# Cross-attention over 1500 keys: key tiles walked in pairs, the turned maxima between two attended tiles, one addition fewer on GpSimd

## What is computed

```python
def sdpa(q, k, v, causal):
    scale = 1.0 / np.sqrt(q.shape[-1])
    scores = jnp.einsum('bhqd,bhkd->bhqk', q * scale, k)
    p = jax.nn.softmax(scores.astype(jnp.float32), axis=-1).astype(q.dtype)
    return jnp.einsum('bhqk,bhkd->bhqd', p, v)
```

## Time and profile before

| what | value |
|---|---|
| median of 3 runs | 1476.83 us (1475.7 to 1477.4) |
| the profiled execution's own time | 1476.38 us |
| its span in the trace | 1474.6 us |
| PE busy over the span | 1403.8 us, 95% |
| DVE, ACT, POOL busy | 906.7, 581.3, 553.7 us |
| the stage that the change touches | from 160.8 to 560.5 us |
| one batch of it, from T to T | 24.52 us, thirteen times out of fifteen |

### The profile page before, as it was taken

The page is one execution under the profiler, slowest core; times in us unless marked ns, Lnnn a source line. Parts: engine busy times, 40 slices in busy tenths (PEclk is TensorE's granted clock), DMA queues, the critical chain, the costliest instruction groups (busy, mean ns, idle before and its releaser), DMA issues.

```text
span 1474.6 us, 20618 instructions
## 1 busy us (share of the span) xinstructions
PE 1403.8 (95%) x7850; PEld 740.6 (50%) x7851; DVE 906.7 (61%) x1429; ACT 581.3 (39%) x880; POOL 553.7 (38%) x385
## 2 busy tenths in 40 slices
PE   6979899999999989998998999999999999999998
PEld 3446555555555544444654455555344355555344
DVE  6896766666667616421226788887433778888540
ACT  1264366666666652001442344444122434444121
POOL 2630388888888891000001144452000144453000
PEclk9999999999999999999999999999999999999999
DMA  7000623232323204004842011110042001110000
GB/s 274 0 2 20 165 70 90 67 92 71 88 66 92 52 13 191 0 0 174 335 124 71 0 39 39 40 39 1 0 122 70 1 27 39 39 39 13 1 0 25
DMA packets 45019, 95.62 MB, mean 65 GB/s; under 512 B 6860, under 2 KB 28892, under 8 KB 44908
## 3 DMA queue, kind: packets, MB, share of 16 engines
q1 hardware_dynamic: 44912, 94.21, 21.0%
HBM read 72.04 MB, written 0.97 MB: 50 GB/s over the span
## 4 chain that ended last, share of the span: by engine, by line
PE 84%; DVE 8%; POOL 3%; issue 2%; ACT 2%; DMA 0%; SPq 0%; DVEq 0%; ACTq 0%; POOLq 0%
PE psum L1658 23%; PE psum L2175 10%; PE psum L1899 5%; PE psum L1875 5%; PE psum L1849 4%; PE psum L2107 4%; PE psum L1832 3%; PE psum L2138 3%; PE psum L1818 3%; POOL XN L708 3%; PE psum L2165 2%; PE psum L2170 2%; DVE WA L1341 2%; PE psum L2167 2%; PE psum L2166 2%
## 5 line engine op out<-in xcount | busy, mean ns | idle before, releaser
L1341 DVE TENSOR_REDUCE WA<-psum 112x2 f32<-112x1000 f32 x192 | 229.8, 1200 | 89.9 <-PE psum L1849 89.9
L708 POOL TENSOR_TENSOR XN<-XN,WBZ 125x896 f32<-125x896 f32 x128 | 266.5, 2082 | 16.8 <-POOL XN L708 0.9
L1052 ACT ACTIVATE WA<-psum,y_bias 125x448 f32<-125x448 f32 x192 | 118.6, 633 | 208.9 <-PE psum L2170 190.4
L933 ACT ACTIVATE WBZ<-psum 125x896 f32<-125x896 f32 x192 | 175.5, 915 | 43.9 <-PE psum L1875 33.3
L2175 PE MATMUL psum<-WA,ctxN 125*128 125x448 f32 x384 | 180.9, 554 | 0.8 <-ACT WA L1052 0.7
L740 POOL TENSOR_TENSOR XN<-const,y_max 112x896 bf16<-112x896 f32 x32 | 75.2, 2350 | 246.2 <-DVE y_max L1557 189.2
L731 POOL TENSOR_SCALAR ctxT<-ctxT 128x375 f32<-128x375 f32 x32 | 56.2, 1756 | 250.9 <-ACT std L806 248.4
L1557 DVE CUSTOM_DVE_ANT_0 XA<-psum,WA 112x375 bf16<-112x375 f32 x240 | 125.3, 541 | 37.6 <-PE psum L2138 36.6
L1875 PE MATMUL psum<-R 100*125 100x224 f16 x768 | 110.7, 266 | 0.0
L1570 DVE RECIPROCAL WBZ<-WBZ 128x224 f32<-128x224 f32 x68 | 105.1, 1546 | 0.1
L1875 PEld LDWEIGHTS psum<-R 100*125 100x125 f16 x768 | 78.9, 136 | 28.3 <-issue 25.0
(11 more groups left out here) (255 smaller groups left out, 2337.9 us busy)
## 6 DMA issues: line engine op xcount, KB each, us to landing
R<-WA SPq DMA_DIRECT2D x192, 93.8 KB, 2.2
WA<-in_ctxT SPq DMA_DIRECT2D x14, 750.0 KB, 4.3
ctxT<-in_ctxT SPq DMA_DIRECT2D x11, 750.0 KB, 4.2
ctxN<-in_ctx SPq DMA_DIRECT2D x32, 192.0 KB, 2.5
ctxT<-in_ctxT SPq DMA_DIRECT2D x32, 187.5 KB, 2.4
R<-in_ctx SPq DMA_DIRECT2D x7, 768.0 KB, 7.3
R<-in_ctxT SPq DMA_DIRECT2D x7, 750.0 KB, 7.2
WA<-in_ctx SPq DMA_DIRECT2D x6, 768.0 KB, 6.4
```

The lines of the kernel that those rows point to most:

```text
L708: nc.gpsimd.tensor_tensor(z_sum[b % 2][0:TK, :], first[0:TK, :], z_p[t % 4][0:TK, :], ALU.add)\
L933: nc.scalar.activation(z_p[t % 4][0:TK, :].rearrange("p (k n) -> p k n", k=2), psum[0:TK, s:s + 2, 0:2 * GC], ACT.Exp, scale=float(CHD0) * ...
L1052: nc.scalar.activation(y_pT[t][0:TK, g * HALF:(g + 1) * HALF], bank[2 + u % 3][0:TK, 0:HALF], ACT.Exp, bias=y_bias[0:TK, bass.ds(b * NT + ...
L1341: V.tensor_reduce(z_mx[0:PR, r:r + 3:2, c], psum[0:PR, lo:lo + 2, 0:PC], AX_X, ALU.max)\
```

## The change

PE now takes two tiles at a time: S of the next two tiles, U, A of tile t, A of tile t+1, and then one piece of V or K whose two halves have the second U between them. In the pair of tiles 8 and 9, T stands between the two A, and both K halves come behind the second U. The four Z of a batch stand directly behind the last A, no longer with a K half in them. POOL adds one tile fewer (SUMS = 8), and PE sums one more (ADDED = 4). POOL's `divide` moves behind the first addition of the next batch. ACT and DVE follow the same pairs.

```diff
-        VALUES_AT = {0: (0, 0), 1: (0, 1), 2: (1, 0), 3: (1, 1), 4: (2, 0), 5: (2, 1)}
-        KEYS_AT = {6: (0, 0), 7: (0, 1), 9: (1, 0), 10: (1, 1), 11: (2, 0), 12: (2, 1)}
+        VALUES_AT = {0: 0, 2: 1, 4: 2}
+        KEYS_AT = {6: 0, 8: 1, 10: 2}
         TURN_AT = 8
-        SUMS = NT - 3
+        SUMS = NT - 4
...
             for b in range(B):
-                if b > 0:
-                    divide(b - 1)
                 if b > 1:
                     pool.wait_ge(sem("z_added"), ADDED * (b - 1))
                 for t in range(1, SUMS + 1):
+                    if b > 0 and t == 2:
+                        divide(b - 1)
...
-                    if b > 0 and t == 3:
+                    if b > 0 and t == 4:
                         quotient(b - 1)
...
             exps(0, 0)
+            exps(0, 1)
             for b in range(B):
...
+                for t in range(0, NT, 2):
+                    for u in (t + 2, t + 3):
+                        if u < NT:
+                            exps(b, u)
+                        elif b + 1 < B:
+                            exps(b + 1, u - NT)
+                        if b + 1 < B and t == TURN_AT and u == t + 2:
+                            shifts(b + 1)
+                    if t + 2 == NT:
+                        evacuate(b)
+                    if b + 1 < B and t in VALUES_AT:
+                        values(b + 1, VALUES_AT[t])
+                    if b + 2 < B and t in KEYS_AT:
+                        high_keys(b + 2, KEYS_AT[t])
...
+                for t in range(0, NT, 2):
+                    for m, k in ahead(b, t) + ahead(b, t + 1):
                         maximum(m, k)
                         if k == UNITS - 1:
                             combine(m)
...
+                    if b + 2 < B and t in KEYS_AT:
+                        low_keys(b + 2, KEYS_AT[t])
+                    if b > 0 and t == 2:
                         invert(b - 1)
...
+            scores(0, 1)
             for b in range(B):
...
+                for t in range(0, NT, 2):
+                    units = ahead(b, t) + ahead(b, t + 1)
+                    for u in (t + 2, t + 3):
+                        if u < NT:
+                            scores(b, u)
+                        elif b + 1 < B:
+                            if b + 1 == EARLY and u == NT:
+                                pe.wait_ge(sem("z_queries1"), STACKED)
+                            scores(b + 1, u - NT)
+                    for m, k in units[0:1]:
                         unit(m, k)
+                    attended(b, t)
                     if b + 1 < B and t == TURN_AT:
                         turn_maxima(b + 1)
...
+                    for m, k in units[1:-1]:
+                        unit(m, k)
+                    attended(b, t + 1)
...
+                    if t + 2 == NT:
+                        for x in range(ADDED):
+                            sums(b, x)
+                    if t == TURN_AT:
+                        for m, k in units[1:][-1:]:
+                            unit(m, k)
+                    for side in range(2):
+                        if b + 1 < B and t in VALUES_AT:
+                            values(b + 1, VALUES_AT[t], side)
+                        if b + 2 < B and t in KEYS_AT:
+                            keys(b + 2, KEYS_AT[t], side)
+                        if side == 0 and t != TURN_AT:
+                            for m, k in units[1:][-1:]:
+                                unit(m, k)
```

More of the change, by code:

```diff
@@ L1373, in _ @@
             for b in range(B):
-                for t in range(NT):
-                    for m, k in ahead(b, t):
+                for t in range(0, NT, 2):
+                    for m, k in ahead(b, t) + ahead(b, t + 1):
                         maximum(m, k)
@@ L1378, in _ @@
                             combine(m)
-                    if b + 2 < B and t in KEYS_AT and KEYS_AT[t][1] == 1:
-                        low_keys(b + 2, KEYS_AT[t][0])
-                    if b > 0 and t == 3:
+                    if b + 2 < B and t in KEYS_AT:
+                        low_keys(b + 2, KEYS_AT[t])
+                    if b > 0 and t == 2:
                         invert(b - 1)
-                if b + 2 < B:
-                    low_keys(b + 2, PIECES - 1)
             invert(B - 1)
@@ L1941, in _ @@
             warm(6, 4)
+            scores(0, 1)
             for b in range(B):
-                for t in range(NT):
-                    for m, k in ahead(b, t)[0:1]:
+                for t in range(0, NT, 2):
[8 more added lines that the diff above has]
+                    for m, k in units[0:1]:
@@ L1962, in _ @@
-                    attended(b, t)
                     if b == B - 1 and t >= COOL:
                         warm(7, 1)
[L1965 to L1969, removed]
+                    for m, k in units[1:-1]:
+                        unit(m, k)
+                    attended(b, t + 1)
+                    if b == B - 1 and t + 1 >= COOL:
+                        warm(7, 1)
```

## The result

The changed kernel took 1467.07 us in the median of four runs (1465.4 to 1470.41), the kernel before 1477.12 beside it: a ratio of 0.9936, 95% interval 0.9917 to 0.9955. Forecast were 1464.5 and 1458.5 to 1471.5. The profiled execution took 1470.41 us, the longest of the four.

A forecast was written before the change was run, and what follows sets the result against it. PE was taken as the bound, busy 24.18 of 24.50 us a batch. Savings of 9.4 + 3.3 - 0.4 = 12.3 us from 1476.38 gave 1464.1; with the median 0.45 above, 1464.5 us, range 1458.5 to 1471.5.

The forecast's parts named there:

- PE sets the pace, by its changes of layout: Steady batch: PE busy 24.18 of 24.50 us; each change between three layouts costs; pairs with V fall from 3.72 to 3.61.
- Pair 8, T at 0.38, in A's layout: Pair of tiles 8 and 9: T between two A shares their layout and costs 0.38 us; pair sum 3.77.
- The rival of a layout of its own: At T between the two A: T's own layout adds 0.20 us a batch, 2.8 in all, 1467.3; chance 0.12.
- an A behind an A takes no more than the price: Denies the rival that A behind A pays like A alone: 0.09 to 0.11 at five places, 1471.5; chance 0.04.
- DVE does not pace the units: Denies the rival that DVE's maxima pace U to U at 1.84, not 1.71: 8.4 us more, 1472.9; chance 0.09.
- Waits at T and behind the low keys, 0.55: Per batch, PE waits 0.13 at T for `low_keys`, and about 0.25 and 0.1 at U in pairs 8 and 0.
- ACT, "Cost nothing": ACT in pair 8, `shifts` between two `exps`, `high_keys` behind: done some 0.4 us before PE asks, so no cost.
- Per batch 0.67, 14 batches 9.4 us: Steady batch: 24.52 less 23.30 and 0.55 of waits saves 0.67 us, over the 14 batches that still make keys.
- POOL no bound, the fourth Z 0.38: POOL's eight additions leave it 18.8 us busy of 23.9; PE's added Z costs 0.38 us a batch.
- The last two batches and the start, 3.3 less 0.4: Last two batches gain 1.7 and 1.6 us, together 3.3, from shorter POOL waits; the stage's start loses 0.4.
- The start, "0.4 lost": Stage start: a second S ahead of the first pair and four units at DVE's 1.71 lose 0.4 us.
- The slower rival (T's chain): T in front of A delays `shifts`, `exps`, `high_keys` and `low_keys`; at 1.4 us a batch, 17.8 more, 1482.3; chance 0.05.

The follow-up runs named there:

- the run with four warm matmuls: Changed kernel plus four matmuls nobody reads, ahead of the two middle U of batch 0's first pair: 1462.40 us, ratio 0.9919 to the kernel before.
- the second measurement: Changed kernel again without any edit, twelve runs beside the kernel before: 1474.47 us against 1475.41, ratio 0.9993.
- the kernel with less warming: Kernel before without the four warm matmuls behind unit(1, 1) at the stage's start: 1483.13 us, ratio 1.0054; once more for its trace, 1491.68 us.
- the kernel with the halves together: Changed kernel with warm matmuls, both halves of V and K together and the second U behind them: 1492.69 us, ratio 1.0116.

## Why the prediction was right, and where it was not

- *PE sets the pace, by its changes of layout*: right. Pairs with V 3.62 against 3.61; A, Z, S and V each within 0.01 of the price, both K halves behind each other 0.92 against 0.94. (The row of K alone that gave the price, is twelve passes, six halves; 0.21 is a pass, and the sum used 0.42 a half, rightly.) The rule of the Trainium skill, TensorEngine Tiling (Array Packing), Key Properties, that a change of mode drains the engine and a change of tile does not, agrees with these rows: an A in front of U or V takes 0.49, an A in front of an A or a Z 0.38 to 0.40.
- *Pair 8, T at 0.38, in A's layout*: right. From T to the following U it is 1.01 us: 0.38, A's 0.49 and a wait of 0.14. The rival of a layout of its own falls. So do two others: an A behind an A takes no more than the price, and the shortest way from U to U is 319.56 - 317.82 = 1.74 us, as summed, so DVE does not pace the units.
- *Waits at T and behind the low keys, 0.55*: 0.05 ahead of T, 0.14 at the U behind it, and 0.06 to 0.08 at the first U of pairs 0, 4 and 8, 0.4 in all. In pair 0 the forecast had it at the second U. Why pairs 4 and 8, which have no low keys shortly ahead, wait there and pairs 2 and 6 do not is not settled. In the program these three U are the first of a piece of keys and wait for one semaphore more (`z_kh`); whether that is the cause, no run shows.
- *ACT, "Cost nothing"*: wrong. K waits 0.27 us a batch for `shifts`, 3.8 us over 14 batches. I had counted ACT's own work in pair 8, and not that K's bank is free only when `shifts` has read T out of it. It is T's own chain again: T 0.05 late, `shifts` 0.91 behind it.
- *Per batch 0.67, 14 batches 9.4 us*: measured 0.54 and 7.5; the wait for `shifts` makes more than the whole difference.
- *POOL no bound, the fourth Z 0.38*: right, both, and shown from both sides.
- *The last two batches and the start, 3.3 less 0.4*: with a full clock at the start (the run with four warm matmuls) the stage fell from 399.7 to 389.3 us; less 7.5 that leaves 2.9, as summed. Counted from last Z to last Z, the last two batches brought 1.0 and 2.0 where 1.7 and 1.6 were forecast, and batch 0, from the first S, brought 0.45, which is 0.1 less than a steady one and not 0.4. The sum is right, its parts are off by 0.3 to 0.7 both ways.
- *The start, "0.4 lost"*: the step that failed. I counted PE's idle time there as time, and not as what it does to the clock. In the first trace it cost 3.7 us, in the second 11.3, as much as the rest of the change brings.
- *The time, 1464.5 us*: 2.6 below the measured median. 1.9 of it is the batch term, 9.4 against 7.5. The clock has at most a small part in that: the profiled execution, which lost 3.7 us to it, is the longest of the four, and its mean clock is 0.989, while the other three have 0.992, as the two shortest of the second measurement do. That the range held was luck in this: in the second measurement nine of twelve executions lie above it, and so does their median, 1474.47. A chance of 0.88 for faster was too high.

The slower rival (T's chain) did not come true in its size, but it named the right chain: it is where the 0.27 goes. The one that was missing is the clock.

## What to carry to other kernels

Where PE is full, write down its groups from start to start with their neighbours: the price of a change of layout is then a row, and a new order can be summed before it is run. Then look where the new order leaves PE idle for the first time after a busy stretch, for a few us of waiting at a start can cost more in clock than the order gains (here 11.3 us in one execution, against 10.4). Four matmuls that nobody reads held it here. And measure more than four executions: here the first four would have hidden it. And take apart a change of several edits: here one edit (the eighth addition) lost 0.38 us a batch under the cover of the others.

## What the runs showed of the hardware that was not expected

- The granted clock fell to its lower level in or right behind a stretch in which PE was idle 0.6 to 1.4 us at a time (busy 5.2 to 5.9 of 8 us), and stayed there for 10 and 27 us and, in the kernel with less warming, some 41 us; another execution of that same kernel did not fall at all. How long it stays down differs between executions of the same instructions, and PE was busy nearly all the while (from 168 to 178 us 9.92 and 10.00 of 10 us, and 9.61 in the kernel with less warming).
- T's four-column fp32 matmuls at partition 96 run beside fp32 matmuls of the other 32-column groups (307.35 and 307.36), but the A of their own group comes behind them, so that T's price stays whole.
- The time from a waiting U to the next, 1.71 us, was the same in the first batch of before and in a steady batch of the kernel with the halves together.
